# A perceiver layer on one core: weight scales moved from VectorE to GpSimd, residual products and the last tile's transposes re-ordered

## The reference, cut to what matters

```python
# x (4,256,256), ctx (4,4096,256)
x = x + cross_attention(layernorm(x), ctx)   # focus + top-k sparsified keys, 16 heads
x = x + cumulative_kv_attention(layernorm(x))   # q * cumsum(k*v) * sigmoid(gate)
x = x + ffn(layernorm(x))

def fake_quant_nvfp4(x, global_scale):       # used on x, hidden and the three weights
    xb = x.reshape(sh[:-1] + (sh[-1] // 16, 16))
    amax = max(abs(xb), axis=-1, keepdims=True)
    sc = clip(amax / 6.0 * global_scale, 0.0, 448.0)
    sc8 = sc.astype(float8_e4m3fn).astype(float32)
    dq = sc8 / global_scale
    safe_dq = where(dq == 0.0, 1.0, dq)
    q = sign(xb) * FP4_VALS[digitize(clip(abs(xb) / safe_dq, 0.0, 6.0), FP4_MIDS)]
    return (q * dq).reshape(sh)

def nvfp4_linear(x, w, s_in):                # s_w = 448 * 6 / max(abs(w))
    return einsum('bsh,oh->bso', fake_quant_nvfp4(x, s_in), fake_quant_nvfp4(w, s_w))

hidden = silu(nvfp4_linear(x, gate_w, s_in)) * nvfp4_linear(x, up_w, s_in)   # 1024 wide
ffn = nvfp4_linear(hidden, down_w, s_in_down)
```

## Time and profile before

| | |
|---|---|
| median of 3 runs | 482.53 us (481.84 to 482.94) |
| the profiled execution | 481.86 us, of which the span of its instructions is 480.1 us |
| busy share of the span | DVE 94%, PE 80%, ACT 75%, POOL 2% |
| chain that ended last | DVE 73%, PE 9%, issue 9%, ACT 7%, DMA 1% |

### The profile page before, as it was taken

How to read it: one execution, slowest core, us unless ns; L and a number is a source line. 1 busy time by engine, 2 the same in 40 slices (tenths; PEclk the granted TensorE clock), 3 DMA queues, 4 the chain that set the end, 5 groups by cost and what they waited for, 6 DMA issues and landing times.

```text
span 480.1 us, 5971 instructions
## 1 busy us (share of the span) xinstructions
PE 383.1 (80%) x1877; PEld 303.2 (63%) x1880; DVE 449.7 (94%) x706; ACT 361.4 (75%) x952; POOL 7.4 (2%) x22
## 2 busy tenths in 40 slices
PE   2996649998998988997897997991999789537764
PEld 1875537787776876886786885891885445213343
DVE  6699999999999999999999999999998879899993
ACT  2469986997997987997887988976438568666764
POOL 2001000000000000000000000000000000000000
PEclk9999879999999999999999999997899999958878
DMA  7933100230220230140140140041010000000001
GB/s 232 354 115 120 55 1 1 87 89 1 88 88 1 69 107 2 50 126 1 46 131 1 42 129 6 1 127 49 13 76 0 1 2 0 1 0 1 23 22 44
DMA packets 27070, 27.65 MB, mean 58 GB/s; under 512 B 1184, under 2 KB 26784, under 8 KB 27040
## 3 DMA queue, kind: packets, MB, share of 16 engines
q1 hardware_dynamic: 26464, 27.00, 17.9%
q10 hardware_dynamic: 416, 0.26, 0.2%
q0 software_dynamic: 160, 0.01, 0.0%
HBM read 26.22 MB, written 1.05 MB: 57 GB/s over the span
## 4 chain that ended last, share of the span: by engine, by line
DVE 73%; PE 9%; issue 9%; ACT 7%; DMA 1%; SPq 0%; ACTq 0%
DVE focus_words L1296 8%; DVE focus_words L1280 8%; DVE sorted L1319 4%; DVE level L1305 4%; DVE level L1306 4%; DVE sorted L1320 4%; DVE merge L1332 4%; PE bank L811 4%; DVE sorted L1197 3%; DVE amax L1166 2%; DVE sorted L1325 2%; DVE sorted L1324 2%; DVE keymax L1322 2%; DVE merge L1330 2%; DVE rank L1343 1%
## 5 line engine op out<-in xcount | busy, mean ns | idle before, releaser
L811 PE MATMUL bank<-WkT,rows_T 128*128 128x256 f32 x512 | 125.2, 391 | 33.5 <-ACT rows_T L429 33.5
L811 PEld LDWEIGHTS bank<-WkT,rows_T 128*128 128x128 f32 x512 | 95.3, 194 | 50.5 <-ACT rows_T L429 39.2
L908 PE MATMUL bank<-ctx_words,focus_words 128*128 128x257 f32 x512 | 115.3, 383 | 3.5 <-ACT focus_words L528 3.5
L908 PEld LDWEIGHTS bank<-ctx_words,focus_words 128*128 128x128 f32 x512 | 99.5, 197 | 16.1 <-ACT focus_words L528 5.5
L516 ACT ACTIVATE focus_words<-focus_words,shift,ff 128x256 f32<-128x256 f32 x136 | 79.8, 590 | 0.6
L482 ACT ACTIVATE focus_words<-bank 128x256 f32<-128x256 f32 x136 | 50.2, 381 | 28.8 <-PE bank L811 28.8
L528 ACT ACTIVATE focus_words<-focus_words,row_scale 128x256 f32<-128x256 f32 x136 | 56.2, 512 | 11.6 <-DVE row_scale L1298 11.6
L429 ACT ACTIVATE rows_T<-bank 128x512 f32<-128x512 f32 x78 | 44.2, 595 | 17.5 <-PE bank L783 17.5
L783 PE MATMUL bank<-ident,ctx_words 128*128 128x128 f32 x256 | 38.2, 278 | 3.5 <-DMA ctx_words<-in_ctx_dram 2.8
L1363 DVE TENSOR_TENSOR mask<-focus_words,fifth 128x2048 bf16<-128x2048 f32 x17 | 39.0, 2292 | 0.5
L783 PEld LDWEIGHTS bank<-ident,ctx_words 128*128 128x128 f32 x256 | 31.6, 144 | 11.5 <-DMA ctx_words<-in_ctx_dram 5.2
(11 more groups left out here) (198 smaller groups left out, 584.1 us busy)
## 6 DMA issues: line engine op xcount, KB each, us to landing
ctx_words<-in_ctx_dram SPq DMA_DIRECT2D x32, 512.0 KB, 4.0
ctx_words<-in_L_ffn_gate_w_dram SPq DMA_DIRECT2D x2, 1024.0 KB, 8.4
ctx_words<-in_L_ffn_up_w_dram SPq DMA_DIRECT2D x2, 1024.0 KB, 9.3
xs<-in_x_dram SPq DMA_DIRECT2D x4, 256.0 KB, 5.6
ctx_words<-in_L_ffn_down_w_dram SPq DMA_DIRECT2D x2, 512.0 KB, 9.7
ctx_words<-in_L_ffn_down_w_dram SPq DMA_DIRECT2D x1, 1024.0 KB, 4.9
out_dram<-xs SPq DMA_DIRECT2D x3, 256.0 KB, 2.1
gateT<-in_L_attn_W_qkv_dram SPq DMA_DIRECT2D x1, 512.0 KB, 6.2
```

Source lines behind the costliest of these rows:

```text
L811: ins = pe.matmul(proj_bank[m][:, t * D:(t + 1) * D], rows_T[:, m % 2, 2 * t + k, :], WT[:, k, :], start=(k == 0), stop=(k == KT - 1))
L908: ins = pe.matmul(sum_bank[k][:, 0:GW], heads_half(expo[slot][:, t, :], k), ctx_ring[:, s, t, :], start=(s == 0 and t == 0), stop=(s == PE ...
```

## The change

Two parts, independent of each other.

**Weight scales.** DVE keeps four small instructions (`tensor_scales`), which now stand at the head of the loop's second pair (a = 3). The other instructions of `weight_scales` and the first two of `weight_reciprocals` are POOL's, between its reduction over the partitions and its transfer of the bias row. DVE's `weight_reciprocals` waits for POOL's last. `out_undo` is made of two products instead of a reciprocal.

**FFN.** The residual product is a function of its own, `residual(t)`. It stands ahead of the transposes of its chunk; in the last chunk that of tile 7 stands between the transposes of tile 6 and those of tile 7. In the last chunk the transposes of tile 7 go half to their usual bank and half to `bank[0]`; ACT copies the first half, and DVE, in one new instruction at its end, the second.

```diff
@@ gpsimd, after partition_all_reduce
             pool.wait_ge(small_loaded, 64)
+            pool.wait_ge(w_scale_ready, 1)
+            pool.tensor_scalar(in_sixth[:, :], in_scale[:, :], 1.0 / FP4_MAX, None, ALU.mult).then_inc(pstep, 1)
...
+            pool.tensor_scalar(out_undo[:, :], w_scale[:, 2:3], in_scale[:, 1:2], 1.0 / UNITS_LEFT,
+                               ALU.mult, ALU.mult).then_inc(pstep, 1)
+            pool.wait_ge(pstep, 7)
+            pool.tensor_scalar(ident_out[:, :], ident[:, :], out_undo[:, 0:1], None, ALU.mult).then_inc(ident_out_ready, 1)
+            pool.tensor_tensor(w_amax[:, :, :], w_amax[:, :, :], each(w_sixth), ALU.mult).then_inc(pstep, 1)
+            pool.wait_ge(pstep, 8)
+            pool.tensor_scalar(w_amax[:, :, :], w_amax[:, :, :], FP8_MAX, None, ALU.min).then_inc(pstep, 1)
+            pool.wait_ge(pstep, 9)
+            pool.tensor_scalar(flat_w(w_magic), flat_w(w_amax), FP8_MAGIC, FP8_LEAST, ALU.mult, ALU.max).then_inc(pstep, 1)
+            pool.wait_ge(pstep, 10)
+            pool.tensor_tensor(flat_w(w_amax), flat_w(w_amax), flat_w(w_magic), ALU.add).then_inc(pstep, 1)
+            pool.wait_ge(pstep, 11)
+            pool.tensor_tensor(flat_w(w_fp8), flat_w(w_amax), flat_w(w_magic), ALU.subtract).then_inc(w_fp8_ready, 1)
+            pool.wait_ge(w_fp8_ready, 1)
+            pool.tensor_tensor(w_rcp[:, :, :], w_fp8[:, :, :], each(w_undo), ALU.mult).then_inc(pstep, 1)
+            pool.wait_ge(pstep, 12)
+            pool.tensor_scalar(w_rcp[:, :, :], w_rcp[:, :, :], TINY / HALF_WAY, None, ALU.max).then_inc(w_undone, 1)
             pool.wait_ge(quad_in_sbuf, group_quad(ATT_BEHIND[1] + 1, 0))
             pool.dma_start(WattT[P - 1:P, KT - 1, :], bias_row).then_inc(bias_row_ready, 16)
@@ scalar, hidden_oct(t)
-                act.activation(hid_fp4T[:, t % 2, :, :], oct_bank[t % 2][:, :].bitcast(BF16).rearrange("p (k c) -> p k c", k=8),
+                blocks = slice(0, 4 if t == T - 1 else 8)
+                act.activation(hid_fp4T[:, t % 2, blocks, :],
+                               oct_bank[t % 2][:, :].bitcast(BF16).rearrange("p (k c) -> p k c", k=8)[:, blocks],
@@ tensor
+            def residual(t):
 
                 c = t // 2
                 if c >= 2:
                     pe.wait_ge(rows_out_ready, c - (t < T - 1))
-                pe.matmul(dst, ident_out[:, :], xs[:, t, :], start=True, stop=False)
+                pe.matmul(down_dst(t), ident_out[:, :], xs[:, t, :], start=True, stop=False)
...
+                more = c + 1 < CHUNKS
+                residual(2 * c)
                 hidden_oct(2 * c)
+                if not more:
+                    residual(2 * c + 1)
                 hidden_oct(2 * c + 1)
                 down(2 * c)
+                if more:
+                    residual(2 * c + 1)
                 down(2 * c + 1)
@@ vector
+            def tensor_scales():
+
+                dve.wait_ge(small_loaded, 64)
+                dve.wait_ge(absmax_reduced, 1)
+                step(dve.reciprocal(in_scale_inv[:, :], in_scale[:, :]))
+                then(dve.reciprocal(w_scale[:, :], w_absmax_all[:, :]))
+                then(dve.tensor_scalar(w_scale[:, :], w_scale[:, :], FP8_MAX * FP4_MAX, None, ALU.mult))
+                dve.reciprocal(w_scale_inv[:, :], w_scale[:, :]).then_inc(w_scale_ready, 1)
...
             def pair(a, last):
...
+                if a == 3:
+                    tensor_scales()
                 compare_pairs(a)
...
-                settle()
-                then(dve.tensor_tensor(w_rcp[:, :, :], w_fp8[:, :, :], each(w_undo), ALU.mult))
-                then(dve.tensor_scalar(w_rcp[:, :, :], w_rcp[:, :, :], TINY / HALF_WAY, None, ALU.max))
+                dve.wait_ge(w_undone, 1)
                 then(dve.reciprocal(w_rcp[:, :, :], w_rcp[:, :, :]))
...
             mix(1)
-            weight_scales()
             mix(2)
...
+            dve.wait_ge(oct_in_psum, FFN_OCTS + 2 + T)
+            dve.tensor_copy(hid_fp4T[:, (T - 1) % 2, 4:8, :],
+                            last_half_bank[:, :].bitcast(BF16)[:, 0:4 * P].rearrange("p (k c) -> p k c", k=4))\
+                .then_inc(last_oct_half, 1)
```

More of the change, by code:

```diff
@@ L81, in perceiver_layer @@
         oct_bank = bank[6:8]
+        last_half_bank = bank[0]
         ctx_words = sb("ctx_words", [P, PER_BATCH * T * GW])
@@ L220, in perceiver_layer @@
         w_max_taken = sem("w_max_taken")
+        w_scale_ready = sem("w_scale_ready")
+        pstep = sem("pstep")
+        w_fp8_ready = sem("w_fp8_ready")
+        w_undone = sem("w_undone")
         front_loaded = [sem(f"front_loaded{s}") for s in range(PER_BATCH)]
@@ L274, in perceiver_layer @@
         ident_out_ready = sem("ident_out_ready")
+        last_oct_half = sem("last_oct_half")
         down_in_psum = sem("down_in_psum")
@@ L282, in perceiver_layer @@
         EVERY, LOWER, UPPER = slice(0, T), slice(0, T // 2), slice(T // 2, T)
+        each = lambda a: a[:, :].rearrange("p (w o) -> p w o", o=1).broadcast_to([P, 3, P])
+        flat_w = lambda a: a[:, :, :].rearrange("p w b -> p (w b)")
         NORM_TILES = (LOWER, UPPER, LOWER, UPPER, LOWER, UPPER)
@@ L410, in _ @@
             pool.wait_ge(small_loaded, 64)
+            pool.wait_ge(w_scale_ready, 1)
+            pool.tensor_scalar(in_sixth[:, :], in_scale[:, :], 1.0 / FP4_MAX, None, ALU.mult).then_inc(pstep, 1)
+            pool.tensor_scalar(in_undo[:, :], in_scale_inv[:, :], NEARLY_ONE / HALF_WAY, None, ALU.mult).then_inc(pstep, 1)
+            pool.tensor_scalar(w_sixth[:, :], w_scale[:, :], 1.0 / FP4_MAX, None, ALU.mult).then_inc(pstep, 1)
+            pool.tensor_scalar(w_undo[:, :], w_scale_inv[:, :], NEARLY_ONE / HALF_WAY, None, ALU.mult).then_inc(pstep, 1)
+            pool.tensor_scalar(out_scale[:, 0:2], w_scale_inv[:, 0:2], in_scale_inv[:, 0:1], UNITS_LEFT,
+                               ALU.mult, ALU.mult).then_inc(pstep, 1)
+            pool.tensor_scalar(out_scale[:, 2:3], w_scale_inv[:, 2:3], in_scale_inv[:, 1:2], UNITS_LEFT,
+                               ALU.mult, ALU.mult).then_inc(pstep, 1)
+            pool.tensor_scalar(out_undo[:, :], w_scale[:, 2:3], in_scale[:, 1:2], 1.0 / UNITS_LEFT,
+                               ALU.mult, ALU.mult).then_inc(pstep, 1)
+            pool.wait_ge(pstep, 7)
[13 more added lines that the diff above has]
+            pool.tensor_scalar(w_rcp[:, :, :], w_rcp[:, :, :], TINY / HALF_WAY, None, ALU.max).then_inc(w_undone, 1)
             pool.wait_ge(quad_in_sbuf, group_quad(ATT_BEHIND[1] + 1, 0))
@@ L622, in spread_fp8 @@
             def spread_fp8(i, dst, fp8):
-                act.wait_ge(fp8_rounded, max(i - 1, 1))
+                if i < 3:
+                    act.wait_ge(w_fp8_ready, 1)
+                else:
+                    act.wait_ge(fp8_rounded, i - 2)
                 act.activation(dst.rearrange("p (b j) -> p b j", j=16),
@@ L1038, in hidden_oct, with down_dst, down @@
                     at = (t % 2) * HIDDEN + b * P
-                    ins = pe.transpose(oct_bank[t % 2][:, :].bitcast(BF16)[:, b * P:(b + 1) * P],
+                    dst, col = (last_half_bank, b - 4) if t == T - 1 and b >= 4 else (oct_bank[t % 2], b)
+                    ins = pe.transpose(dst[:, :].bitcast(BF16)[:, col * P:(col + 1) * P],
                                        hid_fp4[:, at:at + P], ident_b[:, :])
                 ins.then_inc(oct_in_psum, 1)
-            def down(t):
+            def down_dst(t):
+                return (bank[4] if t == T - 1 else bank[4 + t // 2 % 2])[:, (t % 2) * D:(t % 2 + 1) * D]
+            def residual(t):
                 c = t // 2
-                dst = (bank[4] if t == T - 1 else bank[4 + c % 2])[:, (t % 2) * D:(t % 2 + 1) * D]
                 if c >= 2:
                     pe.wait_ge(rows_out_ready, c - (t < T - 1))
-                pe.matmul(dst, ident_out[:, :], xs[:, t, :], start=True, stop=False)
+                pe.matmul(down_dst(t), ident_out[:, :], xs[:, t, :], start=True, stop=False)
+            def down(t):
                 pe.wait_ge(oct_in_sbuf, FFN_OCTS + 2 + t + 1)
                 for k in range(HIDDEN // P):
-                    ins = pe.matmul(dst, hid_fp4T[:, t % 2, k, :], downT[:, k, :], start=False, stop=(k == HIDDEN // P - 1))
+                    if t == T - 1 and k == 4:
+                        pe.wait_ge(last_oct_half, 1)
+                    ins = pe.matmul(down_dst(t), hid_fp4T[:, t % 2, k, :], downT[:, k, :], start=False,
+                                    stop=(k == HIDDEN // P - 1))
                 ins.then_inc(down_in_psum, 1)
```

## The result

The changed kernel takes 483.37 us in the median of 20 runs (482.16 to 484.77), the kernel before 482.41 us in 20 runs beside them. The ratio is 1.0019, 95% interval 1.001 to 1.0028: slower by 0.5 to 1.4 us, where 1.2 us less was forecast. The profiled execution took 483.42 us, with a span of 481.7 against 480.1.

The account below looks back on a forecast made before the run. DVE was taken to bound the loop, PE's order the stretch behind it, and PE alone the FFN's end. +0.53 - 0.73 + 0 + 0 - 1.0 = -1.2 us, from 482.53 to 481.3 us; range for 8 in 10: 479.7 to 487.0.

Parts of the forecast that it names:

- part 3: POOL's 15 instructions beside the loop: all hidden, without holding up DVE, 0 us.
- POOL holds up DVE: Rival, loop's second pair: each POOL instruction delays DVE by its length, 4.5 to 11.5 us, near 486 us; chance 0.33.
- only some instructions collide: Rival, loop's second pair: some POOL instructions hold up DVE, 0.5 to 2.2 us, total 481.8 to 483.5; chance 0.14.
- The row from which the zero was taken: POOL's reduction at 45.66, 2.37 us, beside a two-input DVE instruction of usual length: taken as no hold-up, 0 us.
- The bounds of 4.5 and 11.5 us: Length of POOL's 15 instructions: lower from the same work on DVE, upper from an affine select scaled to 384 columns.
- the prediction's other estimate, near 5: Length of POOL's 15 instructions by the GPSIMD reference's cycles per element: near 5 us.
- Part 1: Four small DVE instructions in the loop, at full price since DVE has no hole: +0.53 us.
- Part 2: Behind the loop: 5.03 us leave DVE's list, but PE's order caps the gain at the mixed_quad(2) transposes: -0.73 us.
- The forecast wait before `key_values(3)` of 3 us: Behind the loop: DVE waits there for PE about 3 us instead of 0.57 or so.
- Part 4: FFN's first three chunks: residual product ahead of transposes delays ACT by up to 0.43 us, covered by 1.4 slack: 0.
- Part 5: Last FFN chunk: both residual products leave the end, the down products run without gap: -1.0 us.
- The clock staying high throughout: Rival, last FFN chunk: PE's clock stays high, -2.4 us in all, 480.1 us; chance 0.12.

Follow-up runs that it names:

- e1: The kernel before with only the weight-scale part of the change, the FFN as before: 484.77 us against 482.28, ratio 1.0051.
- e6: The changed kernel with POOL's seven 384-column instructions given back to DVE, its eight narrow ones left in the loop: 479.71 us in one run, against 482.14 for the kernel before.
- e7: The kernel before plus eight POOL multiplications of two float32 tensors, 384 columns, at the head of the loop's second pair: 488.07 us against 482.14, one run.
- e8: The kernel before plus eight POOL memsets of 384 columns at the head of the loop's second pair: 481.70 us against 482.14, one run.
- e5: The changed kernel with the four small DVE instructions and POOL's 15 moved behind the loop: 479.62 us against 482.14 for the kernel before, ratio 0.9955.
- e3: The kernel before with two lines exchanged, mix(2) ahead of weight_scales(): 481.19 us, ratio 0.9979.
- e2: The kernel before with only the FFN part of the change: 481.19 us, ratio 0.9969.
- e4: The kernel before with the FFN part of the change and mix(2) exchanged to stand ahead of weight_scales(): 480.61 us, ratio 0.9961.

## Why the prediction was wrong

The step that failed is part 3, "I take **0** from it": the price of POOL's work beside the loop. It measured +2.73 us in the changed kernel, and that alone turned -1.2 into a loss; e1 with its 1.0051 shows it in many runs. It was the mechanism of the first rival, "POOL holds up DVE", in the form of the second, "only some instructions collide", at a size between the first one's 4.5 and the second one's upper end of 2.2. The row from which the zero was taken, a reduction that reads three columns, is by its width of the kind that e6 showed to be free, and it could say nothing of 384 columns. It was also read at the wrong place: that DVE instruction had begun at 45.44, before POOL's at 45.66, and in the changed kernel a DVE row that had begun before POOL's first wide one kept its length, while the next one was stretched:

```profile
93.39 2.37 DVE L1334 SCALAR_TENSOR_TENSOR focus_words<-focus_words,key_and,key_xor 128x2048 int32<-128x2048 int32 x1
```

The bounds of 4.5 and 11.5 us were sound for POOL's own length, which was 10.6 us behind the loop (the prediction's other estimate, near 5, was low: the products with one input took 1.17 to 1.53 us there), though in the loop it was 21.2. As a price for DVE both were too high: the heaviest instructions stopped DVE for 0.70 us on average, and the change's own with two inputs take 0.83 to 0.92 with DVE mostly idle, but those with one input cost DVE a fifth of their length and the narrow ones nothing.

The Trainium skill, "SBUF — State Buffer", section "Who interferes with whom", said that two-input DVE instructions and GpSimd instructions that read exclude each other, and that writing alone does not collide. The traces agree with both (e7 and e8). A stop for a whole instruction comes near for two inputs (0.68 to 0.81 us in the rows of e7, where the change's own take 0.83 to 0.92 in e5), but not for the rest: one-input products stopped DVE for 0.22 us and took 1.17 beside an idle DVE (e5), and the eight of e6 did not stop it at all.

Part 1, +0.53 us: 0.57 in the changed kernel and 0.56 in e6. Right.

Part 2, -0.73 us: -0.69, with the mechanism as forecast. PE's order is the cap; the other 4.3 of the 5.03 us shortened nothing and became, for the most part, idle time of DVE. e3 shows it from the other side, with the same 21.23 us and nothing taken off DVE. The forecast wait before `key_values(3)` of 3 us was off: it was 1.26 us, and DVE waited 4.5 us in all at these places, with 0.53 before `mix(2)` and 1.32, 0.25 and 1.18 before the three steps of `add_batch`.

Part 4, 0: the stretch from the cut to the last chunk changed by +0.03. Right.

Part 5, -1.0 us: -0.85 in the changed kernel's profile, -1.5 (-0.8 to -2.1) in the runs of e2. The removal of both residual products from the end is as forecast. That the profile's size is so near is partly luck, since two differences cancel: the products began 0.52 us after the start of tile 7's transposes, not 0.82, since these took 0.72 us, not 1.04, at a clock that was still high at first, and then took 3.51 us, not 3.07, because nearly all ran at the low clock, near 1.2 GHz (0.56 until 478.4). In e2 fewer did. From tile 7's transposes to PE's end it was 4.03 us in the changed kernel and 4.04 in e4, but 3.58, 3.60 and 3.47 in e2, e5 and e6, where the clock was low before the transposes and rose earlier. The clock staying high throughout, a rival, was not seen in any of the executions with the FFN part.

With part 3 at its measured 2.73 the sum is 0.57 - 0.69 + 2.73 - 0.85 = +1.8 us. The spans of the two profiles differ by 1.6, since the rest (an earlier first pair, above all) is -0.16. The medians differ by 0.96.

## What to carry to other kernels

Work given to GpSimd is not free beside a VectorE that has no hole: price what it reads, and do not take its idle time for free time. GpSimd instructions that read 384 columns beside two-input VectorE instructions cost VectorE 0.2 to 0.7 us each here, those with two inputs on 128 columns 0.2, those with one input on 1 to 128 columns and memsets nothing; put wide ones where VectorE waits anyway. Before work is taken off an engine, ask who waits for that engine at that place and until when: here an exchange of two lines brought all that the removal of 5 us could.

## What had not been expected of the hardware

GpSimd suffers from the collision far more than VectorE. A product on two columns took 1.01 us in the loop and 0.26 behind it, the whole block 21.2 and 10.6 us, while VectorE lost 2.73. And a stop is not tied to a long VectorE instruction: a float32 product on 4 columns took 0.70 instead of 0.16 us (352.75 in e5), one int32 instruction on 8 columns 0.79 instead of 0.24 (104.11 in the changed kernel).
